# A two-sweep graph network layer: the last product takes one span, ScalarE copies before it clears, and rows of sweep two are formed early

## The chip, the core and the metric

The program runs on one core of one Trainium2 chip. The metric is the device time of one execution in microseconds (us). Three runs of the kernel before took 1710.31, 1710.64 and 1712.77 us, a median of 1710.64 us. Lower is better.

## The reference, cut to what matters

```python
# L0: graph convolution with symmetric norm over 103125 edges, 3125 nodes, 128 features
h    = x @ weight
out  = segment_sum((dinv[src] * dinv[dst])[:, None] * h[src], dst) + bias
x    = layernorm(x + out)
# L1: edge attention; w_ij is the sum of two small MLPs on the edges' features
w_ij = mlp(edge_attr_64) + mlp(edge_attr_32)          # 64 -> 256 -> 128 and 32 -> 256 -> 128, silu
alpha = (q[dst] * w_ij * k[src]).sum(head) / 4 * edge_weight
out  = segment_sum(alpha * v[src], dst) / 16
x    = layernorm(x + out)
```

The edges are sorted by destination. The MLPs read only the edges' features, so they need nothing of the first layer.

## The kernel before, in words

There are 202 groups of 512 edges, taken in 51 units. Two sweeps pass over the units. Each engine has its own program of the same 51 steps, and the order inside a step is written out by hand; semaphores join the engines. On every engine steps 0 to 2 and 43 to 50 stand unrolled, and a loop of five turns of eight steps (3 to 10, and so on up to 42) stands between.

Sweep one does two things. It forms the sum of the first layer's messages into `acc`, and it computes the MLP weights of one group in four, which are stored in DRAM for sweep two (`w_d`). The messages' sum is formed in two ways. Seven tiles of 128 edges a unit (eight in the last) are gathered from `xs_d` by GpSimd's indirect DMAs (L791), and TensorE adds them through one-hot matrices (`sum1`, L1086); VectorE adds the 42 columns to `acc` (`add_window`, L1463). The other edges are counted: VectorE writes two one-hots a tile (L1470, L1471), TensorE multiplies them (`count_batch`, L1110), VectorE adds the 300 counts into `counts` (`add_counts`, L1487). `counts` has three spans of 112 nodes each, 25 blocks deep. After each 36 batches of counts a product follows (`sum_spans`, L1118): 50 matmuls, of 25 blocks and a high and a low part each, multiply `xs_hi` and `xs_lo` with all three spans at once, 336 columns. VectorE adds the three results to `acc` (`add_spans`), and ScalarE clears the three spans (`clear_counts`, L924). Products stand in steps 8, 16, 24, 32, 40, 48 and in the last, 50. There are 225 batches, so the last product has 9 batches to add, which lie in one span.

The MLP: ScalarE rounds the features (`split_hi`, L888), VectorE forms the rest (`split_lo`, L1449), TensorE does layer 1 (L1060, L1062), ScalarE the silu (L896, four pieces), TensorE layer 2 (`layer2`, L1078, two quarters and then two), ScalarE copies the result to `w_sb` (L916) and seeds the bias for the next unit in the same bank (`seed_bias`, L880). ScalarE does in step s: `split_hi(s + 2)`, `silu(s + 1)`, then a clear if s has a product, then the copy of s and the seed of s + 1. VectorE does `split_lo(s + 2)` after the second batch of counts in a step without a product, and in a step with one before the product's sums. TensorE's bank for layer 2 in sweep one is single, so `layer2(s + 1)` waits for the seed.

In the last step TensorE does the product first, then layer 2 with `sum1` in its middle; VectorE adds the three spans, then the last window. After it VectorE forms the rows of sweep two: `base_f` and an element of `small` are multiplied by a flag (L1552, L1553), `rel0` is a difference over 808 columns (L1555), `relrow0` is moved in place over 1024 columns (L1557), and `next_rows` writes `relrow` from it (L1428). Then comes the middle of the kernel: per chunk of four blocks TensorE multiplies `acc` with the first layer's weight (`convolve`, L1158), VectorE adds that to `nodes` (L1591), to which GpSimd has added the bias (L818, after the last sum into `acc`), statistics and norm follow, then transposes, then k and v, which ScalarE copies out of PSUM (L969) and SyncE's queue stores in `kv_d` (L616, seven stores), and then q, which is stored in three parts (L623).

Sweep two gathers rows of `kv_d` by GpSimd's indirect DMAs (L780, 808 of them), 16 a step. GpSimd starts them as soon as the stores of `kv_d` have landed. TensorE and VectorE do the attention and the sums.

Between the sweeps the engines wait for more than the data: ScalarE for the stores of `w_d` (L929) and for the last sum (L930), TensorE for the last copy of `w_sb` (L1149), VectorE for the clearing of the counts (L1549). SyncE's queue waits for the stores of `w_d`, then loads indices and features for a further pass (which the data of this case doesn't make), and then does the first loads of sweep two (L597).

Of the kernel before, what the change touches and what calls it, by code (L numbers as in the profile page):

```python
# [20 lines left out]
WIN = 42  # L21
# [16 lines left out]
WIDE = 112  # L38
SPANS = 3
# [98 lines left out]
def build(nc, x, x_pad, src_idx, src_e, dst_e, dst_row, dst_first, cut_e, rad_t, sph_t, w_l0, b_l0, rad_w0, rad_b0,  # L138
# [18 lines left out]
    MLPS2 = G - UNITS  # L157
    DEG_COLS = 18
# [7 lines left out]
    with ExitStack() as ctx:  # L166
# [194 lines left out]
        s_zero = sem("s_zero")  # L361
        s_tile = sem("s_tile")
# [102 lines left out]

        def groups2(s):

            return [s.sub(4, j, G) for j in range(4) if not s.is_last() or j < 2]
# [8 lines left out]
        def _(sp):  # L477
# [77 lines left out]
            n_pass1, n_pass2 = passes(sp, 1), passes(sp, 2)  # L555
            with sp.Fori(0, n_pass1) as p:
# [5 lines left out]
                for j in range(2):  # L562
                    sp.wait_ge(s_wstore[j], (p + 1) * 16 * ((UNITS + 1 - j) // 2))
                    sp.sem_inc(s_sp_pass, 1)
                head_loads(p + 1)
# [264 lines left out]
        def _(act):  # L830
# [90 lines left out]
            def clear_counts(k):  # L921
                act.wait_ge(s_span, k.tick + 1)
                for j in range(SPANS):
                    act.activation(counts[:, j, :, :], counts[:, j, :, :].bitcast(F32), ACT.Copy, scale=0.0).then_inc(s_zero, 1)  # L924
# [94 lines left out]
        def _(pe):  # L1019
# [69 lines left out]
            def sum1(s):  # L1089
# [4 lines left out]
                if product(s):  # L1094
# [19 lines left out]
            def sum_spans(added):  # L1114
                pe.wait_ge(s_add, added)
                for h in range(NB):
                    for xs in (xs_hi, xs_lo):
                        mm = pe.matmul(span_ps, xs[:, h, :], counts[:, :, h, :], start=(h == 0 and xs is xs_hi),  # L1118
# [3 lines left out]
            def sweep1(s):  # L1122
# [3 lines left out]
                if s.is_last():  # L1126
                    pe.wait_ge(s_acc1, s.tick)
                    sum_spans((s.p + 1) * COUNTED)
                else:
                    count_batch(own[0])  # L1130
                    layer1(s + 1, mlp1)
                    if product(s):
                        pe.wait_ge(s_acc1, s.tick)
                        sum_spans(own[0].tick)
                    count_batch(own[1])
# [8 lines left out]
            with pe.Fori(0, n_pass1) as p:  # L1144
                steps1(pe, sweep1, p)
# [3 lines left out]
                pe.wait_ge(s_wcopy, p * UNITS + UNITS)  # L1149
# [131 lines left out]
        def _(dve):  # L1281
# [121 lines left out]
            n_pass1 = passes(dve, 1)  # L1403

# [55 lines left out]
            def add_window(base, width, ps, s_sum, value, s_acc, tick):  # L1460
                dve.wait_ge(s_sum, value)
                here = acc[:, ds(base, width)]
                dve.tensor_tensor(here, here, ps, ALU.add).then_inc(s_acc, 1)  # L1463
# [26 lines left out]
            def sweep1(s):  # L1490
# [14 lines left out]

                if product(s):
# [27 lines left out]
                for j in range(3, len(own)):  # L1534
                    batch(j)

            def add_spans(k, bases):
                for j in range(SPANS):
                    if j:
                        dve.wait_ge(s_wide, k.tick * SPANS + j)  # L1540
                    add_window(bases[j], WIDE, span_ps[:, j * WIDE:(j + 1) * WIDE], s_span, k.tick + 1, s_wide, k.tick)
# [10 lines left out]
            v = pre(dve.tensor_scalar(base_f[:, :], base_f[:, :], small[:, 3:4], None, ALU.mult))  # L1552
# [331 lines left out]
```

## Time and profile before

| | us |
|---|---|
| median of three runs | 1710.64 |
| the profiled execution | 1711.38 |
| its span, first to last instruction | 1709.6 |
| TensorE busy | 1540.7 (90%) |
| VectorE busy | 1363.4 (80%) |
| GpSimd busy | 1208.0 (71%) |
| ScalarE busy | 955.3 (56%) |
| sweep one | about 87 to 597 |
| the middle | about 597 to 655 |
| sweep two | about 637 (gathers) or 652 (TensorE) to 1691 |

The profile covers one execution. Its lines give busy time by engine and by line of the kernel, the idle time ahead of each and what ended it, and a chain of waits followed back from the last instruction. The mean granted TensorE clock was 0.981 of full speed.

### The profile page before, as it was taken

To read this page: it belongs to the slowest core of one execution; us is meant where nothing else is said; L and a number is where in the kernel's file an instruction comes from. 1 tells how busy PE (TensorE), PEld (TensorE's weight loads), DVE (VectorE), ACT (ScalarE), POOL (GpSimd) and SP (SyncE) were. 2 spreads that over 40 slices of the span, in tenths; PEclk is the share of its full clock that TensorE was granted. 3 is DMA by queue.
4 is the path that set the end of the run, shared out by engine and by line. 5 is a ranking of instruction groups with operands and counts; after the bars stand their busy time and mean duration, and the time that the engine had idled before them with its cause. 6 is when DMAs were issued, how large, how long until landed. Compare 5 with 4: busy or idle time off the path is not lost.

```text
span 1709.6 us, 44632 instructions
## 1 busy us (share of the span) xinstructions
PE 1540.7 (90%) x12636; PEld 1422.3 (83%) x12636; DVE 1363.4 (80%) x3810; ACT 955.3 (56%) x1412; POOL 1208.0 (71%) x1201
## 2 busy tenths in 40 slices
PE   4389898989899976999999999999999999999995
PEld 3278787878788865999999999998999999999995
DVE  8987777777778365888888888888888888888886
ACT  3354555545565565666666555555555556556554
POOL 5777666666767427777777777777777777777772
PEclk9999999999999987999999999999999999999998
DMA  3133333333334157676666666666666666666664
GB/s 121 45 105 108 97 93 99 92 109 94 109 95 115 52 154 197 187 192 187 179 186 179 180 182 182 182 184 183 178 178 179 183 183 185 180 180 182 183 193 116
DMA packets 176695, 256.68 MB, mean 150 GB/s; under 512 B 80278, under 2 KB 91213, under 8 KB 176476
## 3 DMA queue, kind: packets, MB, share of 16 engines
q0 software_dynamic: 50240, 129.44, 28.1%
q1 hardware_dynamic: 123100, 124.61, 25.8%
q10 hardware_dynamic: 3264, 1.64, 0.3%
q8 instruction: 29, 0.48, 0.1%
q14 instruction: 62, 0.51, 0.1%
HBM read 232.76 MB, written 22.79 MB: 149 GB/s over the span
## 4 chain that ended last, share of the span: by engine, by line
POOL 31%; PE 27%; issue 16%; DVE 13%; ACT 4%; DVEq 4%; DMA 1%; POOLq 1%; SPq 1%; ACTq 0%
POOL arena L780 31%; PE bank L1078 12%; PE bank L1086 5%; PE bank L1060 3%; PE bank L1118 3%; DVE arena L1318 2%; ACT count L924 2%; DVE key_hot L1471 2%; DVE xsplit L1449 2%; DVE low_hot L1470 2%; DVEq L1455 2%; PE bank L1062 2%; DVE count L1487 1%; PE bank L1110 1%; PE bank L1213 1%
## 5 line engine op out<-in xcount | busy, mean ns | idle before, releaser
L780 POOL DMA_INDIRECT arena<-kv_d,idx x808 | 796.0, 985 | 276.6 <-issue 273.0
L1078 PEld LDWEIGHTS bank<-w,hid 128*128 128x128 f32 x6464 | 782.0, 192 | 32.0 <-issue 8.3
L1078 PE MATMUL bank<-w,hid 128*128 128x128 f32 x6464 | 790.7, 276 | 5.0 <-ACT bank L880 5.0
L896 ACT ACTIVATE hid<-bank,b 128x512 f32<-128x512 f32 x808 | 496.6, 682 | 255.5 <-PE bank L1062 246.3
L791 POOL DMA_INDIRECT arena<-xs_d,idx x358 | 353.5, 988 | 161.8 <-issue 112.9
L1060 PE MATMUL bank<-xsplit,w_hi 128*128 128x512 f32 x808 | 346.9, 440 | 50.0 <-DVE xsplit L1449 26.1
L1449 DVE TENSOR_TENSOR xsplit<-xraw,xsplit 64x256 fp32r<-64x256 f32 x808 | 288.4, 414 | 6.7 <-ACT xsplit L888 0.4
L888 ACT ACTIVATE xsplit<-xraw 64x1024 fp32r<-64x1024 f32 x202 | 211.9, 1050 | 80.4 <-DMA xraw<-in_sph_t 53.5
L1060 PEld LDWEIGHTS bank<-xsplit,w_hi 128*128 128x128 f32 x808 | 155.8, 193 | 83.1 <-ACT hid L896 30.2
L1086 PE MATMUL bank<-onehot,late 128*128 128x126 f32 x1616 | 215.7, 282 | 5.5 <-DVE late L1695 3.5
L1086 PEld LDWEIGHTS bank<-onehot,late 128*128 128x128 f32 x1616 | 193.6, 193 | 8.0 <-DVE late L1695 5.4
L880 ACT ACTIVATE bank<-b_full 128x512 f32<-128x512 f32 x199 | 119.0, 598 | 112.7 <-DVE late L1695 111.0
L1487 DVE TENSOR_TENSOR count<-count,bank 128x300 f32 x225 | 103.8, 461 | 90.6 <-issue 42.1
L1648 DVE TENSOR_SCALAR late<-late,iota_part 126x512 bf16<-126x512 bf16 x202 | 74.5, 369 | 116.7 <-PE bank L1213 113.0
L1062 PE MATMUL bank<-xsplit,w_lo 128*128 128x512 f32 x404 | 163.0, 403 | 0.0
L1657 DVE TENSOR_TENSOR late<-arena,bank 128x512 f32<-128x512 f32 x202 | 137.8, 682 | 8.2 <-PE bank L1213 4.6
L1471 DVE TENSOR_SCALAR key_hot<-iota_key,key 128x300 bf16<-128x300 bf16 x450 | 142.1, 318 | 0.0
L1674 DVE TENSOR_REDUCE red<-late 128x32 f32<-128x512 f32 x202 | 137.2, 679 | 0.1
L916 ACT ACTIVATE w_sb<-bank 128x512 f32<-128x512 f32 x51 | 30.3, 595 | 168.9 <-PE bank L1078 168.9
L1669 DVE TENSOR_TENSOR late<-late,bank 128x512 f32<-128x512 f32 x151 | 103.1, 683 | 26.4 <-PE bank L1078 19.7
L1110 PE MATMUL bank<-key_hot,low_hot 128*128 128x300 bf16 x450 | 90.1, 295 | 36.9 <-DVE count L1487 36.8
L1470 DVE TENSOR_SCALAR low_hot<-iota_key,low_f 128x128 bf16<-128x128 bf16 x450 | 116.8, 260 | 4.5 <-issue 4.5
(159 smaller groups left out, 1364.2 us busy)
## 6 DMA issues: line engine op xcount, KB each, us to landing
xraw<-in_rad_t SPq DMA_DIRECT2D x207, 128.0 KB
xraw<-in_sph_t SPq DMA_DIRECT2D x414, 64.0 KB
late<-relrow_d SPq DMA_DIRECT2D x103, 256.0 KB
w_sb<-w_d SPq DMA_DIRECT2D x52, 256.0 KB
w_d<-w_sb SPq DMA_DIRECT2D x51, 256.0 KB
arena<-kv_d,idx POOLq DMA_INDIRECT x808
arena<-xs_d,idx POOLq DMA_INDIRECT x358
qwin<-q_d SPq DMA_DIRECT2D x101, 31.5 KB
```

The lines of the kernel that those rows point to most:

```text
L780: pool.indirect_dma_start(gath[:, k, t * width:(t + 1) * width], None, table, bass.IndirectOffsetOnAxis(ap=idx[:, pair.slot(4), j * TILES ...
L791: pool.indirect_dma_start(gath1[:, k, at_tile:at_tile + D], None, xs_d, bass.IndirectOffsetOnAxis(ap=idx[:, s.slot(4), t:t + 1], axis=0)). ...
L888: act.activation(xsplit[0:RAD, s.slot(2), :, :], xraw[:, k, :, :], ACT.Copy).then_inc(mlp.s_hi, 1)
L896: act.activation(hid[:, s.slot(2), c, :], hid_ps[s.sub(4, c, 4 * s.total).slot(len(hid_ps))][:, :], ACT.Silu, bias=b0[:, c:c + 1]).then_in ...
L1060: mm = pe.matmul(to, w0_hi[:, m, cols], xsplit[:, b, m, :], start=True, stop=(m == 1))
L1062: mm = pe.matmul(to, w0_lo[:, m, cols], xsplit[:, b, m, :], start=False, stop=True)
L1078: mm = pe.matmul(w_ps[:, t * D:(t + 1) * D], hid[:, b, c, t * P:(t + 1) * P], w1[:, c, :], start=False, stop=(c == 3), skip_group_check=True)
L1086: return pe.matmul(bank[7][:, 0:3 * WIN], rows, onehot[:, b, k:k + 3, :].rearrange("p t n -> p (t n)"), start=(k == 0), stop=(k == n - 1), ...
L1449: last = dve.tensor_tensor(xsplit[RAD:P, b, m, half], xraw[:, k, m, half], xsplit[0:RAD, b, m, half].bitcast(F32), ALU.subtract)
L1470: dve.tensor_scalar(low_hot[:, at_tile + t, :], iota_key[:, KEY0:KEY0 + LO], low_f[:, ds(col, 1)], None, ALU.is_equal)
L1471: last = dve.tensor_scalar(key_hot[:, at_tile + t, :], iota_key[:, :], key[:, ds(col, 1)], None, ALU.is_equal)
L1657: dve.tensor_tensor(prod[:, j, :].rearrange("p (t f) -> p t f", t=TILES), kv(g)[:, :, 0, :], q_ps[j][:, :].rearrange("p (t f) -> p t f", t ...
```

## The change

1. In the last product `sum_spans` takes `LAST_SPANS`, which is 1: its 50 matmuls have 112 columns and not 336, and VectorE adds and ScalarE clears one span.
2. In the last step TensorE does two quarters of layer 2, the sums of the gathered tiles, a third quarter, then the product, then the last quarter. VectorE adds the window first and then the span.
3. In the other product steps ScalarE clears one span ahead of the copy of `w_sb` and the seed, and the other two after them; in the last step it clears after the copy.
4. The first four of the five operations that formed the rows of sweep two stand in `rows_ahead`, at the end of VectorE's step 2 of sweep one. `next_rows` stays behind the sweep.
5. ScalarE, TensorE and VectorE no longer each wait for everything at the sweep's end. Two new semaphores, `s_ready` and `s_sent`, stand at the start of a pass in place of these waits.

```diff
+    LAST_SPANS = -(-(COUNTED - (PRODUCTS - 1) * SPANS * SPAN_BATCHES) // SPAN_BATCHES)
...
+            sp.sem_inc(s_sent, 1)
             with sp.Fori(0, n_pass1) as p:
...
             def sweep1(s):
                 activate(s, mlp1)
-                if product(s):
-                    clear_counts(product(s))
+                if product(s) and not s.is_last():
+                    clear_counts(product(s), range(1))
                 act.wait_ge(mlp1.s_w, s.tick + 1)
...
                     seed_bias(w1_ps[0][:, :], mlp1)
+                if product(s):
+                    clear_counts(product(s), range(0 if s.is_last() else 1, spans_in(product(s))))
...
+            act.sem_inc(s_ready, 1)
             with act.Fori(0, n_pass1) as p:
+                act.wait_ge(s_sent, p + 1)
                 steps1(act, sweep1, p)
-                for j in range(2):
-                    act.wait_ge(s_wstore[j], (p + 1) * 16 * ((UNITS + 1 - j) // 2))
-                act.wait_ge(s_acc1, p * UNITS + UNITS)
+                act.wait_ge(s_zero, (p * PRODUCTS + PRODUCTS) * SPANS)
+                act.wait_ge(s_wcopy, p * UNITS + UNITS)
+                act.sem_inc(s_ready, 1)
...
-            def sum_spans(added):
+            def sum_spans(added, n=SPANS):
                 pe.wait_ge(s_add, added)
                 for h in range(NB):
                     for xs in (xs_hi, xs_lo):
-                        mm = pe.matmul(span_ps, xs[:, h, :], counts[:, :, h, :], ...)
+                        mm = pe.matmul(span_ps[:, 0:n * WIDE], xs[:, h, :], counts[:, 0:n, h, :], ...)
...
                 if s.is_last():
-                    pe.wait_ge(s_acc1, s.tick)
-                    sum_spans((s.p + 1) * COUNTED)
+                    layer2(s, mlp1, w1_ps[0], range(2))
+                    sum1(s)
+                    layer2(s, mlp1, w1_ps[0], range(2, 3))
+                    pe.wait_ge(s_acc1, s.tick + 1)
+                    sum_spans((s.p + 1) * COUNTED, LAST_SPANS)
+                    layer2(s, mlp1, w1_ps[0], range(3, 4))
+                    return
...
             with pe.Fori(0, n_pass1) as p:
+                pe.wait_ge(s_ready, p + 1)
                 steps1(pe, sweep1, p)
                 pe.wait_ge(s_acc1, p * UNITS + UNITS)
                 pe.wait_ge(s_again[0], p + 1)
                 pe.wait_ge(s_wide, (p * PRODUCTS + PRODUCTS) * SPANS)
-                pe.wait_ge(s_wcopy, p * UNITS + UNITS)
...
+                if s.is_last():
+                    span_bases = load(span_i, (product(s) * SPANS).n, LAST_SPANS, NP - 1)
+                    dve.wait_ge(s_acc1, s.tick)
+                    add_window(bases[0], WIN, sum1_ps, s_sum1, s.tick + 1, s_acc1, s.tick)
+                    dve.wait_ge(s_acc1, s.tick + 1)
+                    add_spans(product(s), span_bases)
+                    return
...
+                if s.before(3) and not s.before(2):
+                    rows_ahead(s.p)
+
+            def rows_ahead(p):
+                dve.tensor_scalar(base_f[:, :], base_f[:, :], small[:, 3:4], None, ALU.mult)
+                dve.tensor_scalar(small[0:PAIRS, 4:5], relrow0[:, 0, 0:1], small[0:PAIRS, 3:4], None, ALU.mult)
+                dve.wait_ge(s_ahead, p * 4 + 2)
+                dve.tensor_tensor(by_pair(rel0[:, :]), by_pair(dst_f[:, :]), pair_bcast(base_f[:, :]), ALU.subtract)
+                dve.tensor_scalar(relrow0[:, :, :], relrow0[:, :, :], small[0:PAIRS, 4:5], None, ALU.subtract)
...
             with dve.Fori(0, n_pass1) as p:
+                dve.wait_ge(s_ready, p + 1)
                 start_pass1(p)
                 steps1(dve, sweep1, p)
+                dve.wait_ge(s_ahead, p * 4 + 4)
                 dve.wait_ge(s_wide, (p * PRODUCTS + PRODUCTS) * SPANS)
-                dve.wait_ge(s_zero, (p * PRODUCTS + PRODUCTS) * SPANS)
-            v_off = pre(dve.memset(off[:, :], 0.0))
-            ... (the four operations of rows_ahead, each with its wait)
+            dve.memset(off[:, :], 0.0).then_inc(s_pre, 1)
+            dve.wait_ge(s_pre, pre_done + 1)
             next_rows()
```

## Rows read from the trace of the kernel before

**Rows 1.** The page, part 4: shares of the chain of waits by engine.
```profile
POOL 31%; PE 27%; issue 16%; DVE 13%; ACT 4%; DVEq 4%; DMA 1%; POOLq 1%; SPq 1%; ACTq 0%
```

**Rows 2.** Chain of waits between 1200 and 1500 us: shares by line.
```profile
by line: POOL arena L780 75.0%; issue 22.5%; POOLq L801 1.7%; POOLq L797 0.4%; POOLq L778 0.3%; POOLq L122 0.1%
```

**Rows 3.** Instructions of L780 (ns min/median/max, first to last start), who waited for L616.
```profile
L780 POOL DMA_INDIRECT arena<-kv_d,idx x808: 942/946/1387, 637.7 to 1678.7; - x162
...
  POOL arena L780: 30.7, 1
```

**Rows 4.** Timeline of ScalarE in product step 40: start us, us, instruction [idle before <-releaser].
```profile
414.31 7.39 ACT L924 ACTIVATE count<-count 128x2800 fp32r<-128x2800 f32 x3 [6.23 <-PE bank L1118]
421.61 0.58 ACT L916 ACTIVATE w_sb<-bank 128x512 f32<-128x512 f32 x1
422.22 0.60 ACT L880 ACTIVATE bank<-b_full 128x512 f32<-128x512 f32 x1
422.76 1.04 ACT L888 ACTIVATE xsplit<-xraw 64x1024 fp32r<-64x1024 f32 x1
```

**Rows 5.** Timeline of TensorE, steps 40 to 42.
```profile
417.99 1.95 PE L1078 MATMUL bank<-w,hid 128*128 128x128 f32 x16
...
422.95 2.05 PE L1078 MATMUL bank<-w,hid 128*128 128x128 f32 x16 [0.83 <-ACT bank L880]
...
429.61 0.42 PE L1110 MATMUL bank<-key_hot,low_hot 128*128 128x300 bf16 x2 [0.50 <-DVE count L1487]
```

**Rows 6.** Timeline of VectorE, steps 41 and 42.
```profile
425.06 1.43 DVE L1449 TENSOR_TENSOR xsplit<-xraw,xsplit 64x256 fp32r<-64x256 f32 x4
426.95 0.47 DVE L1487 TENSOR_TENSOR count<-count,bank 128x300 f32 x1 [0.47 <-PE bank L1110]
...
429.00 0.47 DVE L1487 TENSOR_TENSOR count<-count,bank 128x300 f32 x1 [0.35 <-PE bank L1110]
```

**Rows 7.** Chain of waits: start us, us, what; steps 41 to 42.
```profile
428.60 0.27 PE bank L1110 x2
429.00 0.12 DVE count L1487
```

**Rows 8.** Chain of waits, steps 48 and 49.
```profile
561.29 7.72 PE bank L1118 x50
...
579.72 1.56 PE bank L1086 x14
...
581.54 1.78 PE bank L1078 x16
```

**Rows 9.** Timeline of all engines, last step of sweep one and what follows.
```profile
584.07 0.60 ACT L880 ACTIVATE bank<-b_full 128x512 f32<-128x512 f32 x1
...
584.90 0.42 PE L1118 MATMUL bank<-count,xs_hi 128*128 128x336 f32 x1 [1.07 <-DVE count L1487]
...
592.91 7.39 ACT L924 ACTIVATE count<-count 128x2800 fp32r<-128x2800 f32 x3 [8.24 <-PE bank L1118]
...
597.56 9.46 POOL L818 TENSOR_TENSOR nodes<-nodes,b_l_sb 128x512 f32<-128x512 f32 x7 [14.18 <-DVE acc L1463]
...
601.15 2.90 PE L1158 MATMUL bank<-w_l_sb,acc 128*128 128x128 f32 x16 [2.92 <-ACT w_sb L916]
...
606.63 0.60 DVE L1591 SCALAR_TENSOR_TENSOR nodes<-bank,dinv,nodes 128x128 f32<-128x128 f32 x2
```

**Rows 10.** VectorE: the start of step 3, L1434 beside gathers, and both runs of L1428.
```profile
120.60 0.47 DVE L1487 TENSOR_TENSOR count<-count,bank 128x300 f32 x1 [1.52 <-PE bank L1110]
...
L1434 DVE TENSOR_SCALAR rel<-rel,off x1: 622/622/622, 649.1 to 649.1; 128x808 f32<-128x808 f32 x1
...
L1428 DVE TENSOR_SCALAR relrow<-relrow,off x2: 748/1190/1632, 605.1 to 1681.7; 101x1024 bf16<-101x1024 f32 x2
```

**Rows 11.** Timelines of SyncE's queue (the stores of `kv_d`) and of ScalarE (copy for chunk 4).
```profile
620.41 13.81 SPq L616 DMA_DIRECT2D kv_d<-arena  x7
...
629.97 0.58 ACT L969 ACTIVATE arena<-bank 128x512 f32<-128x512 f32 x1
```

More of the change, by code:

```diff
@@ L361, in build @@
         s_zero = sem("s_zero")
+        s_ready = sem("s_ready")
+        s_sent = sem("s_sent")
+        s_ahead = sem("s_ahead")
         s_tile = sem("s_tile")
@@ L919, in sweep1, with clear_counts @@
                     seed_bias(w1_ps[0][:, :], mlp1)
-            def clear_counts(k):
+                if product(s):
+                    clear_counts(product(s), range(0 if s.is_last() else 1, spans_in(product(s))))
+            def clear_counts(k, which):
                 act.wait_ge(s_span, k.tick + 1)
-                for j in range(SPANS):
-                    act.activation(counts[:, j, :, :], counts[:, j, :, :].bitcast(F32), ACT.Copy, scale=0.0).then_inc(s_zero, 1)
+                for j in which:
+                    act.activation(counts[:, j, :, :], counts[:, j, :, :].bitcast(F32), ACT.Copy,
+                                   scale=0.0).then_inc(s_zero, 1 + SPANS - spans_in(k) if j == 0 else 1)
+            act.sem_inc(s_ready, 1)
             with act.Fori(0, n_pass1) as p:
+                act.wait_ge(s_sent, p + 1)
                 steps1(act, sweep1, p)
-                for j in range(2):
-                    act.wait_ge(s_wstore[j], (p + 1) * 16 * ((UNITS + 1 - j) // 2))
-                act.wait_ge(s_acc1, p * UNITS + UNITS)
+                act.wait_ge(s_zero, (p * PRODUCTS + PRODUCTS) * SPANS)
+                act.wait_ge(s_wcopy, p * UNITS + UNITS)
+                act.sem_inc(s_ready, 1)
             def root(c, s_var, s_std):
@@ L1093, in sum1 @@
                     pe.wait_ge(s_acc1, s.tick)
-                if product(s):
+                if product(s) and not s.is_last():
                     pe.wait_ge(s_wide, (product(s).tick + 1) * SPANS)
@@ L1117, in sum_spans @@
                     for xs in (xs_hi, xs_lo):
-                        mm = pe.matmul(span_ps, xs[:, h, :], counts[:, :, h, :], start=(h == 0 and xs is xs_hi),
+                        mm = pe.matmul(span_ps[:, 0:n * WIDE], xs[:, h, :], counts[:, 0:n, h, :], start=(h == 0 and xs is xs_hi),
                                        stop=(h == NB - 1 and xs is xs_lo), skip_group_check=True)
@@ L1126, in sweep1 @@
                 if s.is_last():
-                    pe.wait_ge(s_acc1, s.tick)
-                    sum_spans((s.p + 1) * COUNTED)
[L1129 to L1132, printed above, removed]
-                        pe.wait_ge(s_acc1, s.tick)
-                        sum_spans(own[0].tick)
-                    count_batch(own[1])
+                    layer2(s, mlp1, w1_ps[0], range(2))
[5 more added lines that the diff above has]
+                    return
+                count_batch(own[0])
+                layer1(s + 1, mlp1)
+                if product(s):
+                    pe.wait_ge(s_acc1, s.tick)
+                    sum_spans(own[0].tick)
+                count_batch(own[1])
                 layer2(s, mlp1, w1_ps[0], range(2))
@@ L1403, in _ @@
             n_pass1 = passes(dve, 1)
+            pre_done = done[0]
             def start_pass1(p):
@@ L1458, in load, with add_window @@
                 return values
-            def add_window(base, width, ps, s_sum, value, s_acc, tick):
+            def add_window(base, width, ps, s_sum, value, s_acc, tick, n=1):
                 dve.wait_ge(s_sum, value)
                 here = acc[:, ds(base, width)]
-                dve.tensor_tensor(here, here, ps, ALU.add).then_inc(s_acc, 1)
+                dve.tensor_tensor(here, here, ps, ALU.add).then_inc(s_acc, n)
             def hots(batch):
```

19 lines of the change are left out of this document (10 added, 9 removed).

## The prediction

> **What bounds the kernel now.** I read the page's chain of waits first, then the same chain cut into stretches, then the instructions of single lines, then the timelines of one product step and of the passage between the sweeps.
>
> The chain by engine [rows 1] names GpSimd most, then TensorE, idle issue and VectorE. Cut into stretches it has two parts. From some 900 us on it holds nothing but GpSimd's gathers: between 1200 and 1500 us they have 75.0% and the gap between two of them 22.5% [rows 2]. They run from 637.7 to 1678.7 us, 808 of them, so 1.29 us each, almost without a break [rows 3]. Nothing in the change touches them. Sweep two therefore moves as a block with the moment at which GpSimd may begin, and that moment is set by the landing of the last store of `kv_d`, for which it waited 30.7 us [rows 3]. So whatever the end of sweep one gains reaches the end, as long as the seven stores move with it.
>
> In sweep one TensorE and VectorE release one another: the chain goes from a count on TensorE to an addition of counts on VectorE and on [rows 7]. A delay of VectorE in a step is a delay of the sweep, because TensorE waits for it within a batch or two (it waits 0.50 us for L1487 at 429.61 [rows 5]).
>
> **Edit 3, the clears behind the copy, in the five loop products (steps 8 to 40).** I worked step 40 through; the other four look the same in the timeline. Today ScalarE does three clears, 414.31 on, at 2.43 us from one to the next, and only then the copy at 421.61, the seed and `split_hi` at 422.76 [rows 4]. TensorE waits 0.83 us for the seed [rows 5]. That is what the edit aims at.
>
> After it, the first clear ends at 416.8. The copy needs the end of layer 2, 417.99 + 1.95 = 419.94 [rows 5], and starts at 420.06. With the spacings of rows 4 (0.61, then 0.54) the seed is at 420.67 and done at 421.3, so TensorE's wait of 0.83 us goes. But the two other clears now begin at 421.21 and take 2 x 2.43 us, so `split_hi` starts at 426.08 and ends at 427.12; today it ends at 423.80. What is late next is `split_lo` on VectorE, which today starts at 425.06 with 1.26 us to spare [rows 6]. It starts at 427.2, 2.15 us later. VectorE works in its program's order, and the rest of the step stands behind it. Its next addition (426.95) has today a wait of 0.47 us for TensorE in front, which is now inside the delay: it starts at 428.65, 1.70 us late. The addition of today's 429.00 has a further 0.35 us of wait, now gone, with some 0.1 left: 430.26, so 1.26 us late. TensorE's count at 429.61 waits for exactly this addition [rows 5], and VectorE's next addition follows after its own work. So step 42 starts 1.26 us late on both engines, and TensorE's 0.83 us are lost in waiting. Nothing later gives it back: no product, gather or loop end there waits for something that didn't move. The silus of the next unit are done at 429.5 and layer 1 wants their banks at 431.2, so they cost nothing more.
>
> Cost: 5 x 1.26 = +6.3 us. The bounds: if VectorE's delay were hidden, TensorE's 0.83 us would stay, 5 x -0.83 = -4.2 us; if ScalarE's whole shift of 426.08 - 422.76 = 3.3 us passed, +16.6 us. I take 1.26 since each term of it is a row.
>
> In step 48 no `split_hi` follows (there is no unit 51), and the last step's first product isn't due before the seed of unit 50, which stays near its 584.07 + 0.60 = 584.67 [rows 9]. I count nothing there; the cover is the silus of unit 50, which now end near 583.2, just ahead of the copy that releases the seed.
>
> **Edits 1 and 2, the last step.** Today TensorE starts the product at 584.90. ScalarE begins its three clears at 592.91 for 7.39 us, then copies `w_sb`, and TensorE waits for this copy until 601.15. VectorE waits for the clears, forms the rows, ends `next_rows` (L1428) at 605.1 + 1.63 = 606.7, and L1591 follows at 606.63 (ends and starts overlap a little) [rows 9, 10].
>
> After: layer 2 can start at 584.7, when the seed is there. Per instruction the chain's rows give 1.78 / 16 = 0.111 us for L1078 and 1.56 / 14 = 0.111 for L1086 [rows 8]. Two quarters take 1.78, the eight tiles (16 instructions) 1.78, the third quarter 0.89: 589.15. The last window's sum on VectorE runs beside the third quarter. Then the product with 50 matmuls. At 336 columns one takes 7.72 / 50 = 0.154 us [rows 8]. No row has this type of operand with 112 columns. The bounds are: 0.047 us, if the time falls in proportion to the columns from 0.154 with some floor (7.72 x 1/3 = 2.6 us in all); and 0.222 us, twice 0.111, which a product of 126 columns takes in plain f32 as two instructions (L1086), 11.1 us in all. I take 0.111, the nearest row for one instruction with its own weight load and about as many columns: 5.55 us, so 594.7. The last quarter ends at 595.6, and the first chunk of `convolve` (8 instructions) at 596.5; with 0.25 us until VectorE sees it, L1591 starts at 596.75. VectorE itself is ready before: the span's sum at about 595, the memset, then `next_rows`. GpSimd starts L818 some 0.7 us after the last window's sum, near 589.5, and no longer runs beside VectorE's rows. So L1591 moves from 606.63 to 596.75: -9.9 us. With the bounds it would be -12.8 and -4.3 us.
>
> The Trainium skill ("TensorE: Matmul & The Clock Gate", section "LDWEIGHTS (loading the stationary operand)") puts a weight load at its columns over 1.2 GHz, 107 ns for 128. No run here shows such a load alone. An estimate by it is 5.3 us for the product, a floor that would forbid the gain in proportion to columns, and change the time by 0.2 us.
>
> **Does the middle follow?** SyncE's queue moves less: it waits for the last store of `w_d`, whose copy moves from 592.91 + 7.39 = 600.3 [rows 9] to about 595.8, so -4.5 us. Behind that stand loads and the store of the rows, which move by as much, and the first store of `kv_d`, 620.41 today, becomes 616.0 [rows 11], although its data would be there 9.9 us earlier. The queue catches up: seven issues are short, and the seventh today is issued by 620.41 + 13.81 = 634.2 [rows 11], so it would have to go by 624.3, eight us after 616.0. ScalarE's copy for chunk 4 (629.97 today [rows 11], 620.1 after) needs the store of chunk 0 landed, about 3 us after its issue (the first gather waited for the last store from 634.2 to 637.7 [rows 3, 11]), so 619.0 to 619.5. That holds by half a microsecond or more. I count nothing and keep 2 us for the range.
>
> **Edit 4, the rows in step 2.** Today they stand between the end of the clears (600.3 [rows 9]) and L1428 at 605.1 [rows 10], inside the passage above, so their going is counted. They cost in step 2 what VectorE's step 3 begins later. In the passage these operations were slow: L1428 took 1632 ns there and 748 ns in its other run, at 1681.7 [rows 10]; the difference is that L818 ran on GpSimd beside the first [rows 9]. L1434, 808 columns with gathers beside it, took 622 ns [rows 10]. So in step 2 I take 0.2 + 0.15 + 0.2 (the wait) + 0.95 (L1555, two inputs) + 0.65 (L1557) = 2.1 us. Step 3 begins with register loads; VectorE's engine idles 1.52 us there [rows 10], while the two long operations could run. Net +0.6 us. Bounds: 0 and 4.5 us (uncovered and at the passage's durations).
>
> The rule that fits is in the Trainium skill, "GPSIMD Engine Reference", section "Specifications": GpSimd's SBUF interfaces are shared with VectorE, and instructions with two SBUF inputs or in a two-port mode contend. The two durations of L1428 agree. Taken to gathers as well, whose descriptors GpSimd writes, it would speak against the new place and give +2.9 us in place of +0.6; L1434's row speaks against that.
>
> **Edit 5.** The signals of the first pass stand behind set-up work that ScalarE and SyncE finish before VectorE has split `xs` for the products. I count nothing, from 0 to 0.3 us.
>
> **Sum.** +6.3 + 0.6 - 9.9 = -3.0 us. The profiled execution took 1711.38 us (span 1709.6), so it becomes 1708.4; it lies 0.74 above the median of 1710.64, and on that the forecast is 1707.6 us.
>
> **The rivals.**
> - *The narrow product isn't cheap* (chance 0.23). If its price doesn't fall with the columns (0.154 each) the time is 1709.8; at plain f32's 0.222 it is 1713.2. For it: no row of this type under 336 columns. Against: an instruction of 126 columns takes 0.111 us and one of 336 takes 0.154 [rows 8]. I put it at 1711.5.
> - *VectorE hides the late split* (0.10): the seed's wait goes and stays gone, -4.2 in place of +6.3: 1697.1. For it: the wait of 0.83 us is real, in six steps. Against: the 1.26 us to spare at 425.06 are less than the 3.3 us of the shift.
> - *ScalarE's delay passes whole* (0.12), the slower side. One mechanism: two clears ahead of `split_hi` hold VectorE, then layer 1, in each of five steps. At 3.3 us each, 1710.64 + 16.6 + 0.6 - 9.9 = 1717.9. It turns the sign from 9.3 / 5 = 1.86 us a product. For it: everything behind `split_lo` on VectorE waits with it. Against: two waits of rows 6 absorb 0.8 us.
> - *The stores of `kv_d` come late* (0.05): the ring of four buffers stalls ScalarE by 1 to 2 us, 1709.
>
> **From these to the numbers.** The forecast has 0.50, with its own range 1705.5 to 1709.5. Within 0.2% is 1707.2 to 1714.1, about what a measurement of this kernel can tell from no change. Faster: 0.26 of the forecast's 0.50, the hidden split's 0.10, 0.02 of the rest, 0.38. Slower: 0.08 of the whole delay, 0.05 of the costly product and others, 0.13. The same: 0.49. The range is 1702.5 to 1713.5.
>
> **What would show it.** In the timeline of a product step: L880 right behind L916 near 6 us after the first clear, two L924 behind, and L1449 of the next step with an idle of about 2 us ended by L888; no wait of L1078 for L880. The distance between two products grows by 1.26 us each, 5 us from step 8 to step 40. L1118 in the last step: 5.55 us for 50. From the seed of unit 50 to L1591: 12 us, not 22. I am wrong in the first term if L1449 doesn't idle, in the second if the 50 matmuls take 7 us or more, and in the passage if the distance from L1591 to the first L780 (606.63 to 637.7, 31.1 us [rows 3, 9]) changes by over a microsecond.

## The result and the profile after

The changed kernel took 1720.6 us (median of five runs, 1718.7 to 1724.0); the kernel before, in the same session, 1710.3. The ratio is 1.0054, 95% interval [1.0042, 1.0065]: slower, where 1707.6 and a ratio of 0.998 had been forecast. In a later session it was 1.0023 [1.0008, 1.0039]. The profiled execution after took 1723.98 us (span 1722.2), 12.6 more than the one before. It is the slowest of the five, 3.4 us above their median, and the sum below is about this one execution.

One label of the forecast is wrong: the product of [rows 4 to 7], at 406.40, is the fourth of the five in the loop, so the steps called 40, 41 and 42 there are 32, 33 and 34. The number of products doesn't change with it.

First the sum, from where landmarks stand in the two timelines (first product, product of step 48, end of the seed of unit 50, first chunk of layer 0 on VectorE, first gather of sweep two, end):

```
                                      before   after   change  forecast
start to the first product (step 8)   162.7    165.2    +2.5     +0.6
five distances between products       398.4    413.6   +15.2     +6.3
step 48 to the seed of unit 50         23.5     23.2    -0.4      0
that seed to L1591 (after: L1624)      22.0     12.35   -9.6     -9.9
to the first gather of sweep two       31.1     35.25   +4.2      0
to the end                           1071.9   1072.6    +0.7      0
```

Now the rows. ScalarE after the fourth product (start us, us, instruction, idle before it and its releaser), which answers [rows 4]:

```profile
430.93 0.60 ACT L926 ACTIVATE w_sb<-bank 128x512 f32<-128x512 f32 x1 [3.21 <-PE bank L1093]
431.56 0.60 ACT L890 ACTIVATE bank<-b_full 128x512 f32<-128x512 f32 x1
432.10 4.95 ACT L936 ACTIVATE count<-count 128x2800 fp32r<-128x2800 f32 x2
436.95 1.04 ACT L898 ACTIVATE xsplit<-xraw 64x1024 fp32r<-64x1024 f32 x1
```

Copy and seed come at once, and two clears of 2.48 us stand ahead of `split_hi`, as forecast. VectorE, answering [rows 6]:

```profile
438.02 1.48 DVE L1469 TENSOR_TENSOR xsplit<-xraw,xsplit 64x256 fp32r<-64x256 f32 x4 [1.86 <-ACT xsplit L898]
439.54 0.47 DVE L1507 TENSOR_TENSOR count<-count,bank 128x300 f32 x1
...
441.15 0.46 DVE L1507 TENSOR_TENSOR count<-count,bank 128x300 f32 x1
```

It idles for ScalarE (forecast about 2 us, measured 1.86). TensorE, answering [rows 5]:

```profile
436.44 1.95 PE L1093 MATMUL bank<-w,hid 128*128 128x128 f32 x16
438.22 0.42 PE L1125 MATMUL bank<-key_hot,low_hot 128*128 128x300 bf16 x2
440.15 0.42 PE L1125 MATMUL bank<-key_hot,low_hot 128*128 128x300 bf16 x2 [1.51 <-DVE count L1507]
441.75 0.66 PE L1125 MATMUL bank<-key_hot,low_hot 128*128 128x300 bf16 x2 [1.19 <-DVE count L1507]
442.02 0.81 PE L1075 MATMUL bank<-xsplit,w_hi 128*128 128x512 f32 x1
442.63 0.63 PE L1077 MATMUL bank<-xsplit,w_lo 128*128 128x512 f32 x1
443.06 0.63 PE L1075 MATMUL bank<-xsplit,w_hi 128*128 128x512 f32 x1
```

Two gaps, 1.51 and 1.19 us, where one of 0.50 stood [rows 5]; and behind them a matmul of 512 columns takes 0.63 to 0.81 us. In the step before (431.39 to 432) it took 0.40. The forecast has no term for this: TensorE has fallen to the lower of its two levels. The stretches behind the first product say it directly (columns: us, busy of PE, PEld, DVE, ACT, POOL, granted clock, DMA share, GB/s), the same place of the kernel before in the first line:

```profile
186.20:193.20 7.00, 7.00 (x57) 6.47 (x56) 5.70 (x24) 3.33 (x6) 5.17 (x6) 1.00 0.44 125
...
183.00:190.00 7.00, 4.20 (x36) 3.45 (x34) 5.13 (x19) 6.97 (x9) 5.47 (x6) 0.92 0.28 76
190.00:197.00 7.00, 7.00 (x33) 5.96 (x32) 5.33 (x22) 2.83 (x5) 3.90 (x5) 0.60 0.40 116
197.00:200.50 3.50, 3.50 (x32) 3.36 (x31) 1.81 (x7) 0.39 (x1) 1.46 (x2) 1.00 0.05 13
```

0.60 is mostly half speed (1.2 GHz), 1.00 is 2.4 GHz. TensorE is busy all 7 us from 190 on, with 33 matmuls where the kernel before has 57.

The last step, answering [rows 9]:

```profile
601.37 0.60 ACT L890 ACTIVATE bank<-b_full 128x512 f32<-128x512 f32 x1
...
602.10 2.05 PE L1093 MATMUL bank<-w,hid 128*128 128x128 f32 x16 [1.71 <-ACT bank L890]
...
606.94 0.28 PE L1133 MATMUL bank<-count,rounded 128*128 128x112 f32 x1
607.05 0.28 PE L1133 MATMUL bank<-count,xs_hi 128*128 128x112 f32 x1
...
607.05 8.34 POOL L828 TENSOR_TENSOR nodes<-nodes,b_l_sb 128x512 f32<-128x512 f32 x7 [6.20 <-DVE acc L1483]
...
613.10 0.75 DVE L1448 TENSOR_SCALAR relrow<-relrow,off 101x1024 bf16<-101x1024 f32 x1
...
614.32 0.61 DVE L1624 SCALAR_TENSOR_TENSOR nodes<-bank,dinv,nodes 128x128 f32<-128x128 f32 x2 [0.47 <-PE bank L1177]
```

The narrow matmuls start 0.111 us apart. The passage: SyncE's queue and ScalarE, answering [rows 11], then the end of the chain of waits:

```profile
622.72 0.28 SPq L610 DMA_DIRECT2D relrow_d<-relrow  x1
...
633.32 0.80 SPq L589 DMA_DIRECT2D late<-relrow_d  x2
634.17 12.03 SPq L626 DMA_DIRECT2D kv_d<-arena  x7
...
641.02 1.08 ACT L984 ACTIVATE arena<-bank 128x512 f32<-128x512 f32 x2 [2.44 <-DMA kv_d<-arena]
```
```profile
633.46 0.71 ACT arena L984 x2
634.17 6.83 DMA kv_d<-arena
641.02 0.61 ACT arena L984
641.63 0.14 issue
641.76 3.60 PE bank L1196 x10
```

ScalarE waits for the landing of the first `kv_d` store, 6.83 us after its issue. In the kernel before this store landed 5.06 us after its issue, and no wait stood there.

### The profile page after: what moved, and what is told of

Read it like the earlier page. It is cut to its first block, busy times and chain, and to the rows that moved or that the text cites. A ratio compares the mean times of both kernels' runs of the same rounds, so it can differ in the third digit from the quotient of the medians.

```text
span 1722.2 us, 44625 instructions
## 1 busy us (share of the span) xinstructions
PE 1551.3 (90%) x12636; PEld 1431.1 (83%) x12636; DVE 1361.0 (79%) x3808; ACT 951.5 (55%) x1410; POOL 1207.4 (70%) x1201
## 4 chain that ended last, share of the span: by engine, by line
PE 32%; POOL 29%; issue 16%; DVE 11%; DVEq 3%; ACT 3%; DMA 3%; SPq 1%; POOLq 1%; ACTq 0%
POOL arena L790 29%; PE bank L1093 14%; PE bank L1101 5%; PE bank L1075 4%; PE bank L1133 3%; DVE arena L1337 2%; PE bank L1125 2%; PE bank L1077 2%; DVE xsplit L1469 2%; DVEq L1475 2%; DVE key_hot L1491 1%; DVE count L1507 1%; DVE low_hot L1490 1%; ACT count L936 1%; DMA xraw<-in_sph_t 1%
## 5 line engine op out<-in xcount | busy, mean ns | idle before, releaser
L1075 PE MATMUL bank<-xsplit,w_hi 128*128 128x512 f32 x808 | 352.2, 447 | 49.8 <-DVE xsplit L1469 25.6
```

The costliest lines, as they stand in the source:

```text
L1075: mm = pe.matmul(to, w0_hi[:, m, cols], xsplit[:, b, m, :], start=True, stop=(m == 1))
```

## The experiments

The theory (T1): the late clears delay VectorE, and the idle this makes on TensorE drops its clock, which costs again. Against it: T2, the delay alone; T3, the rows in step 2 are the main cost. T4 is about the passage.

Every kernel was timed beside the kernel before, in four later sessions: clears_back, only_clears, rows_back and kv_first in one; after_again (the changed kernel once more), busy_tensor, clears_spread and spread_rows_kv in the next; busy_wide, one_late and spread_rows in the third; one_late_rows_kv in the last. A ratio compares with the kernel before of its own session, so a difference of two ratios from different sessions is less sure than one within a session. No run takes edit 1, 2 or 5 out alone; what they did is read from the timelines. I give the ratio, and from the profile the steps that matter, a step being the distance between the first matmul of layer 1 in it and in the next. "P+1" and "P+2" are the two steps behind each of the five products of the loop, "turn" the four steps after the one in which the loop turns, all summed:

```
                   ratio  [95% interval]    loop   P+1   P+2  turn | 48 to gather
before             1                        398.4  48.5  37.9  34.7 |  76.6
after              1.0054 [1.0042, 1.0065]  413.6  55.1  48.3  33.1 |  70.8
after_again        1.0023 [1.0008, 1.0039]  405.4  54.9  42.9  30.3 |  71.4
only_clears        1.0048 [1.0032, 1.0065]  406.2  55.1  42.9  30.3 |  78.4
clears_back        0.9969 [0.9959, 0.9979]  396.9  48.5  37.9  33.3 |  70.3
rows_back          1.0015 [1.0004, 1.0026]  409.8  55.3  45.7  31.6 |  70.5
kv_first           1.0014 [1.0000, 1.0028]  414.7  55.1  48.6  33.0 |  68.0
busy_tensor        0.9992 [0.9981, 1.0003]  405.6  54.9  42.0  30.3 |  68.4
busy_wide          1.0006 [0.9995, 1.0018]  404.7  54.9  37.9  32.8 |  70.4
one_late           0.9928 [0.9914, 0.9942]  393.4  45.7  37.9  31.9 |  68.4
clears_spread      0.9946 [0.9931, 0.9962]  392.5  45.6  37.9  31.9 |  70.4
spread_rows        0.9917 [0.9902, 0.9932]  393.5  45.5  37.9  33.0 |  70.0
spread_rows_kv     0.9914 [0.9899, 0.9929]  395.1  45.6  37.9  33.0 |  67.8
one_late_rows_kv   0.9920 [0.9903, 0.9936]  393.8  45.6  37.9  33.2 |  67.1
```

"Loop" is the first product to the product of step 48, "48 to gather" the product of step 48 to the first gather of sweep two. A whole step of 7.57 us at full clock reads 8.6 to 9.2 or 10.2 where the clock fell in it. Sweep two, the same code in all, took 1069.5 to 1079.0 us from its first gather, so a single span says little, and the verdicts go by ratios. Of after, clears_back, kv_first and spread_rows the profiled execution was the slowest of the kernel's, of one_late the fastest.

**One part undone, one part alone.** clears_back is the changed kernel with the clears ahead again:

```
-                if product(s) and not s.is_last(): clear_counts(product(s), range(1))
+                if product(s) and not s.is_last(): clear_counts(product(s), range(SPANS))
```

> The changed kernel, with all three clears of a product in the loop ahead of the weight copy again. T1 (the late clears hold split_hi, split_lo and the next two batches back by 1.26 us, and the idle TensorE then falls to half clock, which costs as much again): the distances between products return from about 82.7 to 81 and less, 9 to 15 us go from the 15.2 that the five loop products gained, time about 1705 to 1711. T2 (the delay alone): -6.3 us, 1714. T3 (the rows in step 2 are the main cost): no change beyond 1 us, 1720.

0.9969: 14.5 us less than the changed kernel by its first ratio and 9.2 by its second. That is T1's range. The second figure is good to some 3 us either way, so by itself it wouldn't exclude T2's 6.3; the first does. Both steps behind the product are as before the change.

only_clears puts the same edit into the kernel before:

```
+                if product(s) and not s.is_last(3): clear_counts(product(s), range(1, SPANS))   # behind the seed
```

> The kernel before, with one part of the change alone: at the five products in the loop the clears of the second and third span stand behind the weight copy and the seed. T1: +9 to +15 us on the kernel before, 1719 to 1725, with granted-clock half stretches behind each product. T2: +6.3 us, 1716.6. T3: no change.

+8.2 us (5.5 to 11.1): between T1 and T2, and the interval holds both. The steps tell more than the sum. P+1 is 1.27 to 1.38 us longer at all five products: that is the delay, and it is always there. P+2 reads 7.58, 8.73, 7.57, 8.86, 10.17: the clock's cost, which comes or doesn't. Behind the second product it came:

```profile
266.80 0.42 PE L1112 MATMUL bank<-key_hot,low_hot 128*128 128x300 bf16 x2 [1.52 <-DVE count L1489]
268.40 0.66 PE L1112 MATMUL bank<-key_hot,low_hot 128*128 128x300 bf16 x2 [1.18 <-DVE count L1489]
268.69 0.80 PE L1062 MATMUL bank<-xsplit,w_hi 128*128 128x512 f32 x1
```

The turn's steps, 34.7 us before, are all four 7.57 here: falls that used to come there have moved.

**The rows.** rows_back forms them in the passage, as before the change.

> The changed kernel with the rows of sweep two formed in the passage as before. T1: the first product starts 1 to 2.5 us earlier, the passage is about 2 us longer, time within 2 us of the changed kernel. T3: the time falls by most of the 10 us.

1.0015: 6.7 us less than the changed kernel in the first session, but 1.4 less against after_again, so T3 isn't borne out and the size stays open. The timelines give the local prices. In step 2 the rows' operations are nearly as I had them, from 118.85 with 1.00 and 0.75 us for the two long ones:

```profile
119.28 1.00 DVE L1571 TENSOR_TENSOR rel<-dst_f,base_f 128x808 f32<-128x808 f32 x1
120.19 0.75 DVE L1572 TENSOR_SCALAR relrow<-relrow,small 101x1024 f32<-101x1024 f32 x1
121.55 0.47 DVE L1507 TENSOR_TENSOR count<-count,bank 128x300 f32 x1 [0.61 <-issue]
```

The next addition comes 0.95 us later than at [rows 10]. Step 4 then takes 8.92 us in place of 7.57 (9.14 in after_again, 7.57 in rows_back): a fall of the clock again. It doesn't always come: of the eight kernels with the rows in step 2 five show it, with the first product 2.5 to 3.6 us later than in the kernel before, and three don't (clears_back, kv_first, one_late: 7.57 or 7.58), with 0.8 to 1.4 us; none of the six others shows it. In return L1624 comes 2.6 us earlier than in rows_back (38.2 and 35.5 us behind the product of step 48), and the first gather not at all: 70.5 and 70.8. In these profiles edit 4 bought nothing.

**The passage.** kv_first:

```
                load_weights(s)
-                sp.wait_ge(s_relrow, p * 16 + 16)
-                for pair in pairs2(s): load_rows(pair)
...
+                if c == 2: first_rows(0)     # the same wait and loads, behind the third kv store
```

> The changed kernel with SyncE's wait for the stored rows and the two loads behind it moved from ahead of the seven kv stores to behind the third. T4 (SyncE comes late to the first kv store, the back-to-back stores land late, ScalarE and the gathers wait): the first gather comes 2 to 4 us earlier, time about 1717. If the stores were held by ScalarE's copies alone: no change.

The first gather comes 68.0 us behind the product of step 48 in place of 70.8: 2.8 us, inside what T4 asked for. The time was 1715.8 us, about 1717 was expected. SyncE's queue:

```profile
630.66 4.24 SPq L629 DMA_DIRECT2D kv_d<-arena  x3
634.94 2.03 SPq L589 DMA_DIRECT2D late<-relrow_d  x2
637.68 5.15 SPq L629 DMA_DIRECT2D kv_d<-arena  x4
```

Stores start at 630.7 in place of 634.2, the six of 512 KB land after a median 5.2 us in place of 7.1 (3.3 before), and ScalarE waits for none. One profile proves little here. But that wait of ScalarE is there, 1.1 to 2.8 us long, in all eight kernels that have the narrow product, the rows ahead and the old order of SyncE, and in none of the six others. In five of the eight TensorE's mean granted clock over the 22 us ahead of the first gather is 0.92 as well, and layer 0 to gather takes 34.8 to 35.9 us; where it is 1.00, 33.0 to 34.4; in the three with kv_first's order 31.8 to 32.6. So the order alone is worth less than the 2.8 us. The ratio, 1.0014, is inside what after_again leaves open. And why the first store lands late isn't shown. Its issue close to the next two doesn't do it: busy_tensor issues the three at the same distances (626.46, 626.93, 627.48), and the first landed after 5.04 us, where after has 6.83; in kv_first, with only one other store within 3 us, it took 6.59.

**The clock by itself.** after_again is the changed kernel once more, beside the next three.

> The changed kernel itself, timed beside the three below. All theories: 1716 to 1722; the step behind each product takes 11.0 us (9.7 before) and the one after it 8.8 or 10.2 (7.6 before).

1.0023, 5 us better than in its first session, with the loop at 405.4 us in the profile and not 413.6. The delay is the same (54.9); the clock's steps are not. That the clock makes the spread of one and the same kernel shows in kv_first's twelve executions: six took 1710.4 to 1714.0 us at a mean granted clock of 0.979 to 0.983, the other six 1717.7 to 1719.3 at 0.975 to 0.978.

busy_tensor fills the two gaps with matmuls that nobody reads:

```
+                if not s.before(2) and product(s - 2): keep_busy(10)      # ahead of the step's first batch
+                if not s.before(1) and product(s - 1):                    # ahead of the fifth batch
+                    pe.wait_ge(mlp1.s_silu, (s + 1).tick * 4 + 1); keep_busy(13)
+            def keep_busy(n): n x pe.matmul(bank[0][:, 0:50], xs_hi[:, 0, :], xs_hi[:, 1, 0:50], ...)
```

> The changed kernel, with matmuls whose result nobody reads put into TensorE's two idle gaps behind a product (13 ahead of the fifth batch of the step behind it, 10 ahead of the first batch of the next). The delay of 1.3 us a product stays, the idle goes. T1 (the idle lets the clock fall, and the clock costs more than the delay): the step behind a product still takes 11.0 us, the next one 7.6 at full clock, 8 to 10 us less than the changed kernel, about 1711. T2 (the second loss isn't the clock's): both steps stay as they are, or 1 us longer.

By the steps a miss: the gaps are gone from the rows, the falls are not. P+2 reads 8.97, 7.57, 9.05, 7.57, 8.82. By the time it looks better: 1710.9 us, with 0.9992 beside after_again's 1.0023, so 5.3 us less with intervals that don't touch, where 8 to 10 were expected. But the loops of the two profiles are alike (405.6 and 405.4), and their difference lies behind it: 3.0 us up to the first gather, 2.2 in sweep two. Where the other executions gained isn't shown, and so the number doesn't speak for T1.

```profile
187.00:190.00 3.00, 3.00 (x26) 2.84 (x25) 2.97 (x12) 2.97 (x7) 2.39 (x3) 1.00 0.26 66
190.00:195.00 5.00, 4.84 (x24) 3.65 (x24) 4.22 (x20) 3.36 (x5) 3.78 (x5) 0.66 0.52 152
```

A TensorE busy for all of 187 to 190 fell at once afterwards. Either the idle isn't the cause, or these narrow matmuls don't stand in for the work that is missing. busy_wide changes them alone: `keep_busy(5)` and `keep_busy(6)` with `bank[0][:, :]` and `xs_hi[:, 0:4, :]`, 512 columns.

> As busy_tensor (the changed kernel with matmuls that nobody reads in the two gaps behind a product), but with 6 and 5 matmuls of 512 columns at 0.23 us in place of 13 and 10 of 50 columns, which filled the gaps in the records and left four of the five falls of the clock where they were. T1 in the form left (the fall follows what streams through the array, and narrow matmuls stream little): the step after next behind a product takes 7.6 us at all five products, 5 to 8 us less than the changed kernel. If the falls stay with the gaps full of wide matmuls, their cause is not the idle, and T1's second half falls.

P+2 is 7.57 or 7.58 at all five products. The same stretches, and the rows of the gaps:

```profile
187.00:190.00 3.00, 3.00 (x17) 2.13 (x16) 2.97 (x10) 2.97 (x6) 2.21 (x3) 1.00 0.17 44
190.00:195.00 5.00, 4.85 (x32) 3.72 (x32) 4.42 (x20) 3.76 (x6) 3.85 (x4) 1.00 0.54 161
```
```profile
187.59 1.66 PE L1140 MATMUL bank<-xs_hi 128*128 128x512 f32 x6
189.09 0.43 PE L1125 MATMUL bank<-key_hot,low_hot 128*128 128x300 bf16 x2
189.25 1.42 PE L1140 MATMUL bank<-xs_hi 128*128 128x512 f32 x5
190.82 0.42 PE L1125 MATMUL bank<-key_hot,low_hot 128*128 128x300 bf16 x2
191.13 0.49 PE L1075 MATMUL bank<-xsplit,w_hi 128*128 128x512 f32 x1
```

In the five profiles with two late clears and empty gaps 21 of 25 such steps are slow, with the narrow matmuls 3 of 5, with the wide ones none of 5. So the gaps, filled with wide matmuls, no longer bring these falls; between narrow and wide five steps each are little to go by. And the total missed its 5 to 8 us: against after_again it is 2.9 us less, from another session and with overlapping intervals, and it is no better than with the narrow ones (0.9992). Two falls are back at the loop's turns (8.71, 8.98), one stands three steps behind the fourth product (13.75 us where it takes 13.05 to 13.16 behind the first three, granted clock 0.76 from 451 to 458), and the delay is untouched. A fall put off in one place came in another.

**The delay by itself.** one_late keeps one clear behind the copy in place of two (`range(SPANS - 1)` ahead).

> The changed kernel, with only the third clear behind the copy and the first two ahead of it. By the term that the forecast used (split_hi late by 4.95 us of clears against about 2.8 us of VectorE's other work, so 2.15 us late): with one clear of 2.48 us there, split_hi ends before VectorE asks for it. Step behind a product 9.7 us or less in place of 11.0, no half-clock step after it: about as with all clears ahead of the copy, 1706 to 1709. If any late clear costs its share: half of the loss stays, about 1713.

0.9928, better than expected (1700.5 us). The steps behind a product take 9.10 to 9.18 us, where the kernel before had 9.68 to 9.71, and no P+2 is slow. So there is a threshold: `split_hi` 2.43 us earlier is no longer late, and the seed's wait, gone as the edit meant, is worth 0.57 us a product.

clears_spread puts the second and third clear where ScalarE waits for TensorE anyway:

```
+                for back in (1, 2):
+                    if not s.before(back) and product(s - back):
+                        clear_counts(product(s - back), range(back, back + 1))   # ahead of the copy
```

> The changed kernel, with the second and third clear of a product moved one and two steps on, ahead of the weight copy, where ScalarE waited 2.6 and 4.1 us for TensorE. T1: both steps behind a product are as in the kernel before (9.7 and 7.6 us), 12 to 15 us less than the changed kernel, and the same within 1 us as with all clears ahead of the copy, though the 0.83 us wait for the seed in the product's step is gone, because that step's 15.27 us were the same with the wait and without. If the seed wait was on the path: 4 us less than that.

My own guess, no gain from the seed's wait, is refuted, and the other answer, 4 us less than clears_back, holds: 0.9946 against 0.9969, from two sessions and with intervals that just overlap. It shows in two places: P+1 is 2.9 us shorter in all, and product 48 to layer 0 takes 34.8 us in place of 35.9.

```profile
412.32 2.54 ACT L939 ACTIVATE count<-count 128x2800 fp32r<-128x2800 f32 x1 [6.20 <-PE bank L1136]
418.07 0.60 ACT L929 ACTIVATE w_sb<-bank 128x512 f32<-128x512 f32 x1 [3.21 <-PE bank L1096]
...
422.46 2.54 ACT L939 ACTIVATE count<-count 128x2800 fp32r<-128x2800 f32 x1
425.64 0.60 ACT L929 ACTIVATE w_sb<-bank 128x512 f32<-128x512 f32 x1 [0.64 <-PE bank L1096]
```

The clears lie inside waits for TensorE: behind the first 3.21 us of such a wait are left ahead of the copy, behind the second, one step on, 0.64.

**Versions that beat both kernels.** spread_rows adds `rows_ahead` in the last step, between the last window's sum and `add_spans`, where VectorE waits 6.2 us for the product; spread_rows_kv adds kv_first's order.

> The kernel with the clears spread and the rows formed during the last product, but SyncE's order as in the changed kernel. Against clears_spread: first product 1.0 us earlier by VectorE's work alone and up to 2.6 us with the half-clock step behind it gone; passage as there, since SyncE and not VectorE holds it: 1701 to 1702. What then remains to spread_rows_kv (1697.6) is SyncE's order.

> The kernel with the clears spread, the rows of sweep two formed on VectorE during the last product (it waits 6.2 us there) in place of step 2, and SyncE's load of rows behind the third kv store. T1 and T4 together: first product 1.0 to 2.5 us earlier, passage 2 to 3 us shorter than with the clears spread alone: 1702 to 1705, faster than both kernels.

0.9917 and 0.9914, both below the kernel before by 8 to 9 parts in a thousand (14 to 15 us). The first product starts at 162.4 and 161.8, not 165.7, and step 4 is back at 7.57. SyncE's order moves the first gather by 2.2 us in the profiles (70.0 and 67.8) and the ratio by nothing that the intervals can tell.

> The changed kernel with one clear behind the copy in place of two, the rows of sweep two formed on VectorE during the last product, and SyncE's load of rows behind the third kv store. From the parts: step behind a product 9.1 us with no half-clock step after it, as with one late clear alone; first product 1 to 2.5 us earlier than there; first gather 67.9 us after the last product of the loop in place of 68.4. Ratio to the kernel before 0.990 to 0.993, as with the clears spread over three steps: with both, where the first two clears stand makes no difference as long as split_hi is not held.

0.9920: as expected the two ways of placing the clears can't be told apart.

## Why the prediction was wrong

By its own steps:

- *"ScalarE's two clears hold `split_hi`, `split_lo` starts 2.15 us later, step 42 starts 1.26 us late."* Right, and stable: 2.08 us, and 1.26 to 1.38 a product in three kernels (54.9 to 55.1 against 48.5, +6.5 where +6.3 was forecast).
- *"Nothing later gives it back"*, so the delay is the whole cost. This step failed. The idle of 1.51 and 1.19 us is followed by layer 1 at half clock: P+2 costs 0 to 2.7 us a product. Over the loop the five profiles with two late clears are 0.4 to 9.7 us above before plus delay (405.4 to 414.7 against 398.4 + 6.6). That the falls behind a product come from these gaps is what busy_wide supports (none of 5 with the gaps full of wide matmuls) and clears_back and one_late show from the other side (none of 5 each with the gaps gone). The falls at the loop's turns, 1.2 to 1.6 us each in three of four turns before, partly vanish in exchange. I priced the wait on TensorE in time only. In the nearest profile, after_again's, delay and clock came to +7.0 over the loop, against +6.3.
- *Edit 4, +0.6 us.* The delay was 0.95, and where step 4 fell to half clock (+1.4 to +1.6) the first product came 2.5 to 3.6 us late. The bound of 4.5 held it, for another reason: again the clock, which has no term. (rows_back, with no rows in step 2, is 0.7 us late too, so some of this isn't edit 4's.)
- *The last step, -9.9 us.* Right: -9.6, with 50 matmuls at 0.111 us. The estimate by the page's figure (the Trainium skill, "TensorE: Matmul & The Clock Gate", section "LDWEIGHTS (loading the stationary operand)") of 5.3 us agrees with the trace's 5.5 within 5%. The rival of the costly narrow product fell. The lower bound, 0.047 us, doesn't come out of its own working: 7.72 / 3 / 50 is 0.051. Nothing rests on it.
- *The middle follows with 0.* Failed: +4.2 us. The queue came about as I had it (first `kv_d` store 19.85 us behind L1624, forecast 19.25). The mis-sized term is the landing of that store, "about 3 us after its issue": I took it from the last store, of 128 KB, and the first took 6.83 us. ScalarE's copy for chunk 4 waited 2.44 us for it. The trace of the kernel before already had 5.06 us for this very store; with that the forecast's own sum puts the landing at 616.0 + 5.06 = 621.1, a microsecond behind the copy at 620.1. What made 6.83 of 5.06 stays open. The rival "stores come late" had the mechanism, at 1 to 2 us and a chance of 0.05. With kv_first 2.8 us of the 4.2 went. Of the rest TensorE at half clock has some: 3.60 us for the ten L1196 at 641.76, where the ten of the kernel before took 2.61.
- *Contention with GpSimd.* The forecast had VectorE's rows no longer beside GpSimd's L828. Four of the five operations were gone, but L1448 still ran inside it (613.10, while L828 lasts from 607.05 to 615.39), and took 0.75 us all the same; before it took 1.63 beside L818, and in spread_rows_kv 1.76 beside L833. The single instructions, whose spans on GpSimd are rough, give a hint: in after L1448 starts 0.12 us ahead of GpSimd's next one, which then takes 1.76 us in place of 1.28, and in spread_rows_kv it starts 0.06 us behind one. Which of two goes first seems to decide who pays; no run was made for it. The sum didn't change by it.
- *The rival "VectorE hides the late split".* It is true of one late clear and false of two.
- *The rival "ScalarE's delay passes whole", 1717.9 us.* Its number is the nearest to the measured 1720.6, by luck: the delay was 1.3 us a product and not 3.3, and the rest came from the clock, the start and the passage.

The sum: +1.9 (start), +8.9 (loop), -0.4, +0.3 (last step), +4.2 (passage), +0.7 make the 15.6 us between the forecast -3.0 and the +12.6 of the profile. Nearly 9 of them are the loop's clock in this one execution. In after_again's profile, 7.6 us above the one before, the same terms are +2.6, +0.7, -0.4, +0.3, +4.8 and +2.5, and the ratio is 5 us lower. So the passage and the start missed in both, and the loop in one.

Open: why the same kernel falls in one execution at places where it doesn't in another, and why the first `kv_d` store lands late. The four later sessions ran on three different chips; what that does to a ratio isn't shown.

## What to carry to other kernels

A short wait put on TensorE can have two prices: its length, and the work behind it at half clock. Ask for every new gap what the array does just before and after, and look at the granted clock in the stretch behind it. Work that an engine owes to nobody soon, such as a clear, belongs into that engine's own waits, one piece in each: here two in a row behind the copy cost 8 to 15 us against all three ahead of it, and one there gained 7. And price a transfer from the row of that very transfer, not from the last and smallest of its kind.

## What the runs showed of the hardware

- TensorE kept busy with matmuls of 50 columns (13 and 10, 0.112 us from one to the next) had a mean granted clock of 0.66 in the 5 us behind them; with 6 and 5 of 512 columns in the same gaps it stayed at 1.00. One stretch of one execution each.
- float32r matmuls of 112 and of 50 columns, each with a weight load ahead of it, follow one another at 0.111 and 0.112 us, so the narrower ones gained nothing; 336 columns take 0.154, 512 columns 0.23.
- Of seven stores to DRAM the six of 512 KB landed after a median of 7.1 us where the first three were issued within 1.03 us (634.17 to 635.20), and after 3.3 where they went 2.4 and 3.2 us apart (620.41, 622.78, 625.93). The distance isn't all: busy_tensor's first three, issued within 1.02 us, landed after 5.04, 5.92 and 6.72 us, those of after, 6.83, 7.65 and 8.46.
